# Per-engine orders from a list scheduler, separate buffers for the ternary layer, copies on ScalarE and causal masks off TensorE, in a fused attention and ternary feed-forward kernel

## Chip, cores and metric

One core of a Trainium2 chip. The metric is the device time of one execution in microseconds.

## The reference

x is 2048 rows of 256 numbers. With xn the row-normalised x, the result is x + attention(xn) + ffn(xn).

```
q, k, v   = xn @ Wq (8 heads of 32), xn @ Wk, xn @ Wv (2 key/value heads of 32); rope on q and k
out_1     = softmax(causal(q k^T / sqrt(32))) @ v
qp, kp    = q[..., :3] . dirs[h],  k[..., :3] . dirs[h]        (one number per row and head)
out_2     = softmax(causal(qp kp^T)) @ v
attention = (out_1 + head_scale[h] * (out_2 - out_1)) @ Wo

z      = xn @ ternary(W_syn)^T + b_syn          (1024 columns)
hidden = relu(z) where z >= the 102nd largest z of its row, else 0
ffn    = layernorm(xn + hidden @ ternary(W_out)^T + b_out) * gamma + beta
ternary(W) = clip(round(W / mean|W|), -1, 1) * mean|W|
```

## The kernel before

The 2048 rows are 16 tiles of 128 rows, and 4 chunks of 4 tiles. Per chunk c there is a preparation, a search for the row maxima of the scores, and the attention.

Preparation. VectorE's `row_stats` takes mean and variance of four tiles, GpSimd raises to the power -0.5 (L478), VectorE normalises (L651). Per tile TensorE transposes xn (L897), projects to q, k, v (L904), VectorE applies rope from PSUM (L679 to L688), splits q and k into a rounded and a rest part so that fast single-pass matmuls keep the precision (L693 to L706), TensorE transposes them (L909 to L915), ScalarE copies q (L567) and VectorE k (L713, L715) into the stacks. `geo` (from L720) computes running maxima for the second softmax and SP's queue spreads its rows by 16 small DMAs (L409, L412).

Maxima. The softmax needs the row maximum before the exponential. For tile t, head h, piece p a unit S computes scores of 128 rows against up to 512 keys into PSUM (L925); the last piece, which holds the diagonal, gets a further matmul that adds a mask of -1e30 (L928); VectorE reduces the unit (L745). There are 320 units, c+1 pieces for each of 8 heads and 4 tiles of chunk c. The maxima are transposed (L933) and go by DMA into a row of the q stack, so that the scores' matmul subtracts them itself.

Attention. A slot is (chunk, key/value head g, kind, key tile j): kind 0 is the first softmax, kind 1 the geometric one. Per slot TensorE computes the transposed scores of 4 heads, two pairs of PSUM banks (kind 0 at L1006, kind 1 at L1009); in a diagonal slot a mask matmul follows per head (L1013); ScalarE takes the exponential of a pair (L552) into one of two buffers `probs`; TensorE multiplies by v and by ones (L1027) into `acc`. After the last j of a kind an epilogue follows: ScalarE copies the sums (L559), VectorE the values (L770), takes a reciprocal (L772), GpSimd mixes (L503 to L510). The output projection is L984, added at L778.

Ternary layer. W_syn, later W_out, come into `z_work`, which rope's intermediates, z of tile 0 and the work space share; L785 sums |W|, L794 and L795 cut to -1, 0, 1, and the result is transposed and copied (L952, L806). Per tile t: transpose and split of xn (L956, L817, L818), z in two halves (L962 to L964), ScalarE copies with relu and sum (L582), three rounds of Sign with sum search a threshold that leaves the 102nd value within 16 ranks (L597 to L612), VectorE finds it (`select`, L825 to L834), a branch on the count of rows found (a slow path if any row missed, L857), masks (L860), transposes (L970), split (ScalarE L588, VectorE L868), down matmuls (L976, L977), layer norm on VectorE and GpSimd (L875 to L879, L523 to L529).

All units but scores and acc go through the two PSUM banks of `side`, strictly in turn: unit n uses bank n mod 2 and waits until unit n-2 has been read. `build_plan` writes one list, which every engine walks for its share in the same order. It simulates three clocks with durations written in it. `side` is a fixed list (all chunks' preparation and maxima, then weights, then the ternary layer), `slots` the attention. A side unit is placed when its bank is free on TensorE's clock plus `EARLY`, otherwise the next attention step. `blocked` holds chunk c's statistics back until chunk c-2 has been attended.

## Time and profile before

| what | us |
|---|---|
| median of 3 runs | 963.46 |
| the runs | 953.23, 963.80, 963.46 |
| profiled execution, device time | 967.53 |
| its span, first to last instruction | 965.7 |
| TensorE matmul busy | 810.1 (84%), mean granted clock 0.853 |
| TensorE weight loads | 417.4 (43%) |
| VectorE busy | 578.8 (60%) |
| ScalarE busy | 417.8 (43%) |
| GpSimd busy | 152.6 (16%) |

Busy times are sums over instructions; overlapped ones count once. Matmuls are pipelined and their ends are modelled, so the distance between two starts says more than a duration. A granted clock of 1.0 is 2.4 GHz, 0.5 is 1.2 GHz.

### The profile page before, as it was taken

Reading aid. Unit: us, or ns where it says so; the run is one execution under the profiler, and the core shown is the slowest. Engines: PE = TensorE matmul, PEld = TensorE weight load, DVE = VectorE, ACT = ScalarE, POOL = GpSimd, SP = SyncE. Lnnn points to the kernel's source line nnn. Section 1 sums busy time; section 2 is a strip of 40 time slices with the busy share of each in tenths; the row PEclk is TensorE's granted clock in tenths of the full one; section 3 lists DMA queues with packets and bytes.
Section 4 is the critical chain, followed back from the end, with each engine's and each line's share of the span. In section 5 each row is a group of like instructions: output and inputs, shape, how many; then the busy total and the mean of one; then the engine's idle time right before and its main releaser. Section 6 shows DMA issues by size and latency. Waiting matters only on the chain.

```text
span 965.7 us, 12678 instructions
## 1 busy us (share of the span) xinstructions
PE 810.1 (84%) x4916; PEld 417.4 (43%) x4916; DVE 578.8 (60%) x1139; ACT 417.8 (43%) x657; POOL 152.6 (16%) x162
## 2 busy tenths in 40 slices
PE   1677995779999997999999976889899999899643
PEld 0364554534444442543444423345445445344333
DVE  5467376675567776456587844536656654655652
ACT  0102440004543424462143352378787678676430
POOL 4000022000002002000020000200232423222443
PEclk9756797557999897998699897899899899799965
DMA  5000000000000000000000002000000000000000
GB/s 153 0 1 6 2 1 1 0 1 6 1 1 1 1 1 8 1 1 1 1 1 1 1 8 75 14 1 1 7 12 7 6 7 12 6 6 6 6 7 17
DMA packets 12436, 9.40 MB, mean 10 GB/s; under 512 B 5778, under 2 KB 11794, under 8 KB 12371
## 3 DMA queue, kind: packets, MB, share of 16 engines
q1 hardware_dynamic: 12242, 8.49, 3.0%
q8 instruction: 39, 0.64, 0.3%
q14 instruction: 27, 0.21, 0.1%
q0 software_dynamic: 128, 0.07, 0.1%
HBM read 5.80 MB, written 2.10 MB: 8 GB/s over the span
## 4 chain that ended last, share of the span: by engine, by line
PE 55%; DVE 13%; ACT 9%; issue 5%; DMA 1%; SPq 1%; POOL 0%; DVEq 0%; POOLq 0%; ACTq 0%
PE acc L1027 20%; PE side L925 10%; ACT probs L552 5%; PE scores L1006 5%; DVE piece_max L745 4%; PE scores L1009 3%; PE scores L1013 2%; PE side L984 2%; PE side L962 2%; PE side L976 2%; PE side L977 1%; PE side L963 1%; PE side L904 1%; DVE h_split L868 1%; PE side L909 1%
## 5 line engine op out<-in xcount | busy, mean ns | idle before, releaser
L552 ACT ACTIVATE probs<-scores 128x1024 f32<-128x1024 f32 (+3 forms) x320 | 275.9, 897 | 403.9 <-PE scores L1013 205.5
L745 DVE TENSOR_REDUCE piece_max<-side 128x1 f32<-128x512 f32 (+3 forms) x320 | 184.4, 607 | 79.5 <-PE side L925 47.4
L1027 PE MATMUL acc<-probs,v_nat 128*32 128x512 f32 (+3 forms) x1280 | 163.7, 585 | 12.0 <-DVE o_raw L770 8.0
L925 PE MATMUL side<-k_stack,q_stack 96*128 96x512 f32 (+3 forms) x320 | 148.0, 513 | 18.6 <-DVE piece_max L745 13.4
L1027 PE MATMUL acc<-probs,ones 128*32 128x512 f32 (+3 forms) x1280 | 159.6, 572 | 0.0
L1006 PE MATMUL scores<-q_stack,k_stack 98*128 98x512 f32 (+3 forms) x320 | 103.3, 423 | 17.3 <-DMA q_stack<-maxima 13.9
L925 PEld LDWEIGHTS side<-k_stack,q_stack 96*128 96x128 f32 x320 | 69.3, 226 | 104.9 <-DVE piece_max L745 77.4
L1006 PEld LDWEIGHTS scores<-q_stack,k_stack 98*128 98x128 f32 x320 | 56.8, 205 | 62.9 <-issue 30.8
L1009 PE MATMUL scores<-q_geo,k_geo 5*128 5x512 f32 (+3 forms) x320 | 66.1, 493 | 7.5 <-ACT probs L552 5.2
L1027 PEld LDWEIGHTS acc<-probs,ones 128*32 128x32 f32 x1280 | 36.6, 115 | 65.8 <-issue 63.4
L868 DVE TENSOR_TENSOR h_split<-side,h_split 128x512 fp32r<-128x512 f32 x32 | 20.9, 687 | 62.2 <-ACT h_split L588 61.8
L772 DVE RECIPROCAL d_raw<-d_raw 128x512 f32<-128x512 f32 x16 | 53.6, 3353 | 7.3 <-ACT d_raw L559 6.9
L1009 PEld LDWEIGHTS scores<-q_geo,k_geo 5*128 5x128 f32 x320 | 27.2, 193 | 65.7 <-issue 37.2
L1013 PE MATMUL scores<-mask_r,ident_r 128*128 128x128 f32 x256 | 53.7, 293 | 0.0
L1013 PEld LDWEIGHTS scores<-mask_r,ident_r 128*128 128x128 f32 x256 | 43.9, 203 | 13.4 <-issue 8.5
L1027 PEld LDWEIGHTS acc<-probs,v_nat 128*32 128x32 f32 x1280 | 26.4, 111 | 51.5 <-issue 38.2
L523 POOL TENSOR_TENSOR y_rstd<-y_mv,minus_half 128x1 f32<-128x1 f32 x16 | 9.0, 563 | 222.6 <-DVE y_mv L879 222.6
L567 ACT CAST q_stack<-side 96x512 fp32r<-96x512 f32 x32 | 17.6, 583 | 59.6 <-PE side L909 59.6
L507 POOL TENSOR_TENSOR o_raw<-o_raw,d_raw 128x512 f32<-128x512 f32 x8 | 10.1, 1268 | 201.9 <-DVE d_raw L772 201.9
L970 PE MATMUL side<-ident,z_work 128*128 128x128 f32 x128 | 20.6, 313 | 23.2 <-DVE z_work L860 23.2
L909 PE MATMUL side<-ident,q_nat 128*96 128x128 f32 x128 | 21.4, 321 | 22.0 <-DVE geo_nat L706 21.8
L503 POOL TENSOR_TENSOR mixed<-o_raw,d_raw 128x512 f32<-128x512 f32 x8 | 10.2, 1269 | 172.8 <-DVE d_raw L772 172.7
(166 smaller groups left out, 1068.3 us busy)
## 6 DMA issues: line engine op xcount, KB each, us to landing
res<-in_L_attn_x_dram SPq DMA_DIRECT2D x4, 512.0 KB, 7.0
out_dram<-res SPq DMA_DIRECT2D x16, 128.0 KB, 1.7
z_work<-in_L_ffn_W_syn_dram SPq DMA_DIRECT2D x1, 1024.0 KB, 5.2
z_work<-in_L_ffn_W_out_dram SPq DMA_DIRECT2D x1, 1024.0 KB, 4.8
k_geo<-geo_split SPq DMA_DIRECT2D x24, 8.0 KB
q_geo<-geo_split SPq DMA_DIRECT2D x24, 8.0 KB
w_qkv<-in_L_attn_Wq_dram SPq DMA_DIRECT2D x1, 256.0 KB, 4.4
tables<-in_cos_table_dram SPq DMA_DIRECT2D x1, 256.0 KB, 4.6
```

The lines of the kernel that those rows point to most:

```text
L552: nc.scalar.activation(probs[:, slot % 2, pair, :, off:], scores[:, pair, :, off:], ACT.Exp, scale=ATT_SCALE if kind == 0 else 1.0).then_i ...
L745: free(nc.vector.tensor_reduce(piece_max[:, h, p:p + 1], pt[:, 0:ncol], AX.X, ALU.max), a)
L772: nc.vector.reciprocal(d_raw[:], d_raw[:]).then_inc(recip_ready, 1)
L868: free(nc.vector.tensor_tensor(h_lo[:, s_], pt, h_hi[:, s_].bitcast(F32), ALU.subtract), a)
L909: last = nc.tensor.transpose(pt[0:STK, P * i:P * i + P], q_nat[:, 4 * half + i].bitcast(F32), ident[:])
L925: last = nc.tensor.matmul(pt[:, 0:ncol], q_stack[0:STK, b, h, col:col + P], k_stack[0:STK, h // HG, CHUNK * p:CHUNK * p + ncol], start=Tru ...
L962: nc.tensor.matmul(pt, xs_hi[:, i], up_T[:, i, cols], start=(i == 0), stop=False)
L970: last = nc.tensor.transpose(pt[:, P * i:P * i + P], work[:, at:at + P], ident[:])
L1006: last = nc.tensor.matmul(dst[:, off:], k_stack[:, g, P * j:P * j + P], q_stack[:, b, HG * g + h, off:], start=True, stop=not diagonal)
L1009: last = nc.tensor.matmul(dst[:, off:], k_geo[32 * h:32 * h + GROWS, g, P * j:P * j + P], q_geo[32 * h:32 * h + GROWS, b, g, off:], start= ...
L1013: last = nc.tensor.matmul(scores[:, pair, i, off:off + P], ident_r[:], mask_r[:, 0], start=False, stop=True)
L1027: last = nc.tensor.matmul(acc[D * h:D * h + D, 0 if k == "values" else 1, off:], lhs, probs[:, slot % 2, h // 2, h % 2, off:], start=first ...
```

## The change

The plan becomes one order per engine (`plan["pe"]`, `"dve"`, `"act"`, `"pool"`, `"sp"`). Work is cut into items; `add(flow, engine, rank, key, ns, after)` gives each a duration and what it needs. Items of one flow and engine keep their order, flows are free against each other. At each step the item that can start first is placed; among those of the same engine within `SLACK` ns the lowest rank wins. Attention has the lowest priority on TensorE (12, 13), picks on VectorE (4, 5); exp, cut and epilogue copies the highest on their engines. Side units take whichever bank is free first, no longer in turn, and a bank is counted with its own semaphore.

- The ternary layer gets own buffers (`z_buf` of three, `work`, `junk`), rope gets `rot` and `xnT`. W_syn is fetched right after the attention weights, ahead of the later x chunks; the layer may begin when its weights are cut.
- ScalarE takes over: the normalisation (`xn`, as scale and shift), the copies of xnT, of q's twin, of k and the geometric rows, `geo_hi`, sum of |W| (Abs with sum, in two halves), the cut weights after their transposition, `xs_hi`.
- GpSimd takes over the geometric dot products (`geo_dots`), the products of `geo_max`, and the causal cut.
- Both mask matmuls go. The scores of a diagonal slot stay unmasked and GpSimd zeroes the exponentials above the diagonal (`cut`, affine_select on 128x256, per pair); the values wait for it. The diagonal S piece is reduced by a tensor_tensor_reduce that adds `tail_mask` from SBUF.
- Values and sums are one item. Both key/value heads' geometric rows lie in one k_geo of 10 rows per head. TensorE waits for all 8 constants at the start.

```diff
-EARLY = 260
+HAND = 160
+TURN = 110
+SLACK = 120
...
+        for t in tiles:
+            old = [("unit", "qT", t - 1, 1), ("unit", "kT", t - 1)] if t else []
+            unit("qkv", 2 * c, ("xT", t), 220, [("xn", t)])
+            add("xnT", "act", 1, ("xnT", t), 400, [("unit", "xT", t)] + [("unit", "qkv", t - 1)] * (t > 0), empties=("xT", t))
+            unit("qkv", 2 * c, ("qkv", t), 1300, [("xnT", t)] + [("w",)] * (t == 0))
+            add("rope", "dve", 0, ("rope", t), 1930, [("unit", "qkv", t)] + [("q_twin", t - 1), ("geo_dots", t - 1)] * (t > 0),
+                empties=("qkv", t))
+            add("rope", "dve", 0, ("split", t), 1350, [("rope", t)] + old)
...
+                    unit("S", 2 * c + 1, ("S", t, h, p), 25 + 0.41 * cols, [("q_in", t, h // HG), ("k_in", t)])
+                    add("S", "dve", 1, ("red", t, h, p), 152 + 1.045 * cols + (20 if p == c else 0), [("unit", "S", t, h, p)],
+                        empties=("S", t, h, p))
...
+        add("pick", "dve", 5, ("pick", t, 0), 1750, [("sign", t, 2)] + [("unit", "hT", t - 1, 1)] * (t > 0))
+        add("pick", "dve", 4, ("hide", t), 2750, [("unit", "found", t)], empties=("found", t))
+        unit("h", 10, ("fo", t), 1900, [("h_lo", t, 0), ("h_lo", t, 1)] + [("w_put", 1, 3)] * (t == 0))
...
+            add("exp", "act", 0, ("exp", c, g, kind, j, pair), 170 + 855 * share, [("score", c, g, kind, j, pair)]
+                + ([("vs",) + slots[n - 2]] if n >= 2 else []))
+            if j >= TPC * c:
+                add("cut", "pool", 0, ("cut", c, g, kind, j, pair), 440, [("exp", c, g, kind, j, pair)])
...
+        add("vs", "pe", 13, ("vs", c, g, kind, j), 60 + 1700 * share,
+            [("cut" if j >= TPC * c else "exp", c, g, kind, j, PAIRS - 1)]
...
+        first = min(b[0] for b in best)
+        close = [b for b in best if b[0] <= first + SLACK and b[3] == min(best)[3]]
+        start, rank, key, eng, flow, ns, m = min(close, key=lambda b: (b[1], b[0]))
...
-                        if not full:
-                            last = nc.tensor.matmul(pt[:, col:col + P], ident_r[:], mask_r[:, 1], start=False, stop=True)
...
+                        free(nc.vector.tensor_tensor_reduce(pt[:, 0:ncol], pt[:, 0:ncol], tail_mask[:, CHUNK - ncol:], 1.0, -3.0e38,
+                                                            ALU.add, ALU.max, piece_max[:, h, p:p + 1]), ("S",) + a)
...
-                    if diagonal:
-                        for i in range(2):
-                            last = nc.tensor.matmul(scores[:, pair, i, off:off + P], ident_r[:], mask_r[:, 0], start=False, stop=True)
...
+                if k == "cut":
+                    c, g, kind, j, pair = a
+                    at = (j - TPC * c) * P
+                    tri = probs[:, slot_no[(c, g, kind, j)] % 2, pair, :, at:at + P]
+                    pool.wait_ge(probs_ready, score_no[a] + 1)
+                    nc.gpsimd.affine_select(out=tri, in_=tri, compare_op=ALU.is_ge, fill=0.0, base=0,
+                                            pattern=[[0, 2], [1, P]], channel_multiplier=-1).then_inc(cut_ready, 1)
...
+                    if j >= TPC * c:
+                        pe.wait_ge(cut_ready, cut_no[a + (PAIRS - 1,)] + 1)
+                    else:
+                        pe.wait_ge(probs_ready, score_no[a + (PAIRS - 1,)] + 1)
...
+                if k == "xn":
+                    t = a[0]
+                    act.wait_ge(shift_ready, t // TPC + 1)
+                    nc.scalar.activation(xn[:, t], res[:, t], ACT.Identity, bias=shift[:, t:t + 1],
+                                         scale=rstd[:, t:t + 1]).then_inc(xn_ready, 1)
```

## Rows read from the trace of the kernel before

**Rows 1.** Busy time by stretch; columns: stretch, length, busy by engine, granted clock, DMA.
```profile
0.00:84.00 84.00, 42.95 (x141) 29.40 (x141) 49.73 (x132) 5.93 (x9) 11.72 (x16) 0.72 0.17 45
84.00:144.00 60.00, 57.43 (x432) 32.15 (x432) 34.26 (x81) 26.08 (x41) 9.80 (x11) 0.86 0.01 3
144.00:218.00 74.00, 49.18 (x140) 32.56 (x140) 52.29 (x99) 2.29 (x4) 6.12 (x5) 0.58 0.00 1
218.00:363.00 145.00, 141.01 (x908) 65.85 (x908) 95.82 (x201) 59.72 (x76) 8.97 (x7) 0.94 0.01 2
363.00:562.00 199.00, 190.26 (x1092) 84.22 (x1096) 126.81 (x245) 77.54 (x92) 15.04 (x12) 0.88 0.01 2
562.00:608.00 46.00, 29.31 (x215) 12.41 (x208) 21.49 (x26) 17.40 (x21) 0.63 (x1) 0.83 0.16 50
608.00:910.00 302.00, 278.86 (x1902) 142.58 (x1902) 171.58 (x311) 220.20 (x398) 75.16 (x84) 0.94 0.02 6
910.00:965.70 55.70, 21.15 (x92) 18.25 (x92) 26.87 (x52) 8.63 (x18) 25.18 (x27) 0.62 0.03 10
```
**Rows 2.** The same for the tile piece_max (maxima), then probs (exponentials), then line L977.
```profile
218.00:363.00 145.00, 56.98 (x100) 0.94 0.01 2
363.00:562.00 199.00, 78.39 (x132) 0.88 0.01 2
...
608.00:910.00 302.00, 125.28 (x1024) 25.47 (x1024) 110.91 (x124) 0.94 0.02 6
...
608.00:910.00 302.00, 25.16 (x104) 19.61 (x104) 0.94 0.02 6
```
**Rows 3.** Timeline of TensorE in the attention of chunk 2: start, duration.
```profile
385.67 1.20 PE L1006 MATMUL scores<-q_stack,k_stack 98*128 98x512 f32 x4
...
388.65 1.20 PE L1006 MATMUL scores<-q_stack,k_stack 98*128 98x512 f32 x4
```
**Rows 4.** Timeline of TensorE around masks and S units in chunk 1.
```profile
341.10 0.44 PE L1013 MATMUL scores<-mask_r,ident_r 128*128 128x128 f32 x2
...
341.37 0.44 PE L925 MATMUL side<-k_stack,q_stack 96*128 96x512 f32 x1
...
344.17 0.73 PE L925 MATMUL side<-k_stack,q_stack 96*128 96x512 f32 x2
...
344.89 1.06 PE L1027 MATMUL acc<-probs,ones 128*32 128x512 f32 x8
```
**Rows 5.** Timeline of the ternary layer beside the attention of chunk 3.
```profile
650.60 0.40 PE L963 MATMUL side<-up_T,xs_lo 128*128 128x512 f32 x1
...
650.84 0.40 PE L964 MATMUL side<-b_up_r,ones_r 65*128 65x512 f32 x1
...
660.73 1.28 DVE L860 SCALAR_TENSOR_TENSOR z_work<-z_work,thresh 128x1024 f32<-128x1024 f32 x1 [1.28 <-DVEq L857]
...
663.44 1.09 PE L970 MATMUL side<-ident,z_work 128*128 128x128 f32 x8
```
**Rows 6.** Timeline of the start on VectorE, and one projection on TensorE.
```profile
9.00 8.63 DVE L651 TENSOR_SCALAR xn<-res,mean_var,rstd 128x256 f32<-128x256 f32 x4 [1.24 <-POOL rstd L478]
...
22.65 0.49 DVE L679 TENSOR_TENSOR z_work<-side,tables 128x320 f32<-128x320 f32 x1 [3.09 <-PE side L904]
...
26.04 0.42 DVE L670 COPY z_work<-side 128x256 f32<-128x256 f32 x1
```
```profile
236.75 1.56 PE L904 MATMUL side<-w_qkv,z_work 128*128 128x384 f32 x4
```
**Rows 7.** Groups of instructions by form: count, busy us, mean ns, idle before.
```profile
L772 DVE RECIPROCAL d_raw<-d_raw 128x512 f32<-128x512 f32 x16 | 53.6, 3353 | 7.3 <-ACT d_raw L559 6.9
...
L466 POOL TENSOR_SCALAR_AFFINE_SELECT xb<-xb 128x128 f32<-128x128 f32 x1 | 0.3, 292 | 0.1
```
**Rows 8.** Timeline at 910 us: VectorE and GpSimd side by side.
```profile
909.79 2.31 DVE L827 SCALAR_TENSOR_TENSOR z_work<-head_rows,search 128x1024 f32<-128x1024 f32 x1
911.10 2.13 POOL L508 TENSOR_TENSOR o_raw<-o_raw,mixed 128x512 f32<-128x512 f32 x1
```

More of the change, by code:

```diff
@@ L88, in build_plan, with add, unit @@
-    alone = {"stats": 3500, "geo": 8500, "mx": 200, "weigh": 4600, "select": 7200}
-    def up(t):
-        return [("up_xs", t), ("up_z", t)]
-    side = []
+    op, queue, ranks = {}, {}, {}
+    def add(flow, eng, rank, key, ns, after=(), mode=None, empties=None):
+        op[key] = (eng, ns, tuple(after), mode, empties)
+        ranks[key] = rank
+        queue.setdefault((eng, flow), []).append(key)
+    def unit(flow, rank, name, ns, after=()):
+        add(flow, "pe", rank, ("unit",) + name, ns, after, "full")
@@ new lines, in build_plan @@
+    for t in range(NT):
+        unit("o", 0, ("o", t), 860, [("mix", t // TPC, G - 1, 1)])
+        add("o", "dve", 0, ("o_add", t), 430, [("unit", "o", t)], empties=("o", t))
+        add("dma", "sp", 0, ("store", t), 500, [("o_add", t), ("y_out", t)])
+    done = {("x", c): 6000 + 1500 * c for c in range(NCH)}
+    done.update({("w",): 9000, ("late",): 14000, ("w_in", 0): 12000, ("w_in", 1): 13000})
+    emptied_by = {}
+    for key, o in op.items():
+        if o[4]:
+            emptied_by.setdefault(o[4], []).append(key)
@@ new lines, in build_plan @@
+    gates = {}
+    for name, keys in emptied_by.items():
+        own, seen = ("unit",) + name, list(keys)
+        for r in seen:
+            seen += [d for d in op[r][2] if d in op and own in op[d][2] and d not in seen]
+        gates[own] = tuple(d for r in seen for d in op[r][2] if d != own and d not in seen)
+    bank = {}
+    holds = [None] * BANKS
+    clock = {e: 0.0 for e in ("pe", "dve", "act", "pool", "sp")}
+    mode = "full"
+    heads = {q: 0 for q in queue}
+    plan = {e: [] for e in clock}
@@ L469, in late_constants @@
[L469 to L490 removed]
+            constant(nc.gpsimd.memset(ones, 1.0))
@@ L1025, in _ @@
-                    for h in range(HG):
-                        lhs = v_nat[:, j, g] if k == "values" else ones[:, 0:D]
-                        last = nc.tensor.matmul(acc[D * h:D * h + D, 0 if k == "values" else 1, off:], lhs,
-                                                probs[:, slot % 2, h // 2, h % 2, off:], start=first, stop=end)
-                    if k == "sums":
-                        last.then_inc(probs_used, 1)
+                    if j >= TPC * c:
+                        pe.wait_ge(cut_ready, cut_no[a + (PAIRS - 1,)] + 1)
+                    else:
+                        pe.wait_ge(probs_ready, score_no[a + (PAIRS - 1,)] + 1)
@@ L1034 @@
+                    if first and e >= 1:
+                        pe.wait_ge(raw_ready, 2 * e)
+                    for part, lhs in enumerate((v_nat[:, j, g], ones[:, 0:D])):
+                        for h in range(HG):
+                            last = nc.tensor.matmul(acc[D * h:D * h + D, part, off:], lhs,
+                                                    probs[:, slot % 2, h // 2, h % 2, off:], start=first, stop=end)
+                    last.then_inc(probs_used, 1)
 _INS = ["L0_attn_x", "L0_attn_Wq", "L0_attn_Wk", "L0_attn_Wv", "L0_attn_Wo", "L0_attn_head_scales", "L0_ffn_W_syn",
```

1078 lines of the change are left out of this document (586 added, 492 removed).

## The prediction

> **What bounds the kernel now.** I read the stretches first. The cuts are mine: 84 us is where the first attention score starts, 144, 363 and 608 lie where the attention of chunk 0, 1 and 2 ends or the next can begin, 910 is the last reciprocal. TensorE shows as busy 810 of 965.7 us, but its instructions are long for two reasons: where the granted clock is low (0.58 to 0.72 of a stretch, a mean of its levels of 1.2 and 2.4 GHz) many take twice as long, and beside other work a matmul's latency is counted as busy. Three things stand out [rows 1].
>
> First, attention is absent for long. It starts at 84 us; from 144 to 218 us ScalarE works for 2.3 us, since the attention of chunk 1 waits for its row maxima and TensorE (clock 0.58) only feeds the reductions; from 562 to 608 us the weights of the ternary layer are fetched and cut; from 910 to 966 us three tiles of the ternary layer go through one after the other, TensorE busy 21 us, clock 0.62. Second, the ternary layer starts only at 608 us: 104 of the 128 down matmuls of one line, 13 of the 16 tiles, lie between 608 and 910, on top of the longest attention [rows 2]. Third, VectorE is busy 579 us, spread at 60% over all of it: the maxima alone are 57 and 78 us in 218-363 and 363-562, 21.4 more for each chunk of 32 more pieces of 512 columns, so 36 in the stretch before and 0.67 us a piece [rows 2]. No engine is full; the order of the work is what costs time. So I price what each stretch needs on each engine, and ask what the new order lets lie side by side.
>
> **Unit prices at full clock.** A full attention slot of kind 0 (scores, values, sums) repeats after 388.65 - 385.67 = 2.98 us; kind 1 has cheaper scores, I take 2.6, so 2.8 on average [rows 3]. Diagonal slots counted by columns, chunk c has 4(4c+2.5) full slots: 10, 26, 42, 58, or 28, 73, 118 and 162 us. Two S units and a mask take 344.89 - 344.17 = 0.72 us with both changes of shape, so 0.3 us a unit without mask [rows 4]; 32, 64, 96, 128 units are 10, 19, 29, 38 us. A projection is 1.56 us, and with its ten transposes (eight take 1.1 us) a tile's preparation is 2.9, a chunk 11.5 us [rows 5, 6]. A ternary tile: ten 512-column matmuls each 0.24 us after the last, eight transposes, and 16 down matmuls of half the columns at 0.12, with xsT 5.7 us [rows 5]. Output projection about 3.5 us a chunk (16 matmuls of 256 columns and 4 passes each).
> VectorE: preparation of a tile 26.04 - 22.65 = 3.4 us, chunk 13 [rows 6]; maxima 15, 36, 57, 78 us; each epilogue 3.35 for the reciprocal and 0.7 for the copy, 16 us a chunk [rows 7]; a ternary tile (171.6 - 16)/13 = 12 us in 608-910 plus 1.3 us standing at the branch [rows 1, 5], so 13.3.
>
> **The edits.** *Masks off TensorE.* Two diagonal masks cost 341.37 - 341.10 = 0.27 us [rows 4], so the 256 are 35 us at full clock; with the 128 S masks about 45. Below: nothing, where VectorE is late; above: twice that at half clock, 90. I take them out by using prices without masks (8 to 10 us a chunk). In return VectorE adds a mask inside the diagonal reduction. The trace has no such instruction; nearest is a reduction of the same PSUM tile, so plus nothing; far bounds are a gain of nothing and the reciprocal's 3353/512 = 6.5 ns a column [rows 7]: 40,960 columns by 5.2 ns more than a piece's 1.3 are 215 us. I take nothing, since two-operand PSUM instructions run like one-operand ones (0.49 us for 320 columns) [rows 6].
> *Cut on GpSimd.* 128 selections of 128x256 on the exponentials. The mask builder takes 0.29 for 128x128 [rows 7]; so 0.3 to 0.6 each, I take 0.45 and 58 us in all. It lies between exp and values in 64 diagonal slots. With two probs buffers the other slot covers it if GpSimd is free; uncovered it is 64 x 0.6 = 38 us. In front of it on GpSimd may stand a mix of four operations (5.7 us) or y_out (4.5); this I keep as a rival.
> *Copies to ScalarE.* Some six 128x256 copies a tile at 0.42 [rows 6] are 40 us, and weights, geometry and small products 30 more: VectorE falls from 579 to about 510, ScalarE rises from 418 to some 470, GpSimd from 153 to about 245. ScalarE has the room: in 608-910 it needs 110.9 for exp and (220.2 - 110.9)/13 = 8.4 a tile [rows 1, 2], so 196 of 245 us after the change. SP's queue gains W_syn ahead of the later x chunks: 5 us, hidden, as these chunks are wanted after 60 us. Values and sums in one item: two changes of shape fewer per slot (up to 160 x 0.2 = 32 us), but VectorE may stand 0.5 us more behind each; I take zero.
>
> **Sum by stretch.**
> Start to first score, 84: the first transpose waits until about 18, because the four normalisations took 8.63 us, where four instructions of the size of L670's 0.42 are 1.7, while GpSimd filled memory [rows 6]; these go to ScalarE and the big fill is late, so first matmul near 11. Tiles overlap (own buffers), 6 us instead of 8 a tile, and the maxima of tile 0 start before tile 3 is ready. 84 - 7 - 8 - 11 = 58.
> 84-218, 134 us: VectorE needs 13 + 36 + 16 + 8 (geometry, statistics) = 73, TensorE 28 + 19 + 11.5 = 59. VectorE bound: 78.
> 218-363, 145 us: TensorE 73 + 29 + 11.5 + 3.5 = 117, VectorE 57 + 13 + 16 + 8 = 94. Two ternary tiles fit: TensorE 128, VectorE 121: 130.
> 363-608, 245 us: TensorE 118 + 38 + 11.5 + 3.5 = 171, VectorE 115, room for four tiles: 194, at clock 0.95: 204.
> 608-910, 302 us: 162 + 3.5 + ten tiles 57 = 223, at 0.95 and 4% of waits: 245.
> Tail, 56 us: reciprocal 3.4, mix 5.7, four projections 3.5, add, store and what the last tile lags: 22.
> 58 + 78 + 130 + 204 + 245 + 22 = 737 us of span. The orders are fixed per engine by a plan at full clock with a hand-over of 160 ns, and the chip's clock will differ; a queue that waits in order loses some of it: 11 us. With 2 us around the span that is **750 us**. The profiled execution took 967.5 (span 965.7), the runs shown have a median of 963.5, 0.4% less; I let that stand inside the range.
>
> **A rule that speaks against the change.** At 909.79 VectorE's L827 with two SBUF inputs took 2.31 us beside GpSimd's L508 with 2.13 [rows 8], against 1.28 of VectorE's L860 of the same form [rows 5]: about 1 us lost per collision. This kernel puts 92 us more on GpSimd. The Trainium skill (SBUF — State Buffer, "Who interferes with whom") says a VectorE instruction with two SBUF inputs and a GpSimd instruction that reads SBUF exclude one another for the whole instruction; by that rule the trace agrees, and nearly every cut that meets a pick waits for it.
>
> **Rivals.**
> *Gaps close, stretches don't shrink* (25%). For: in 218-562 TensorE already shows 331 of 344 us busy, and each S unit between attention matmuls costs two changes of shape; static orders drift. Against: VectorE is busy there only 65%, and there are masks to save. 60 + 90 + 145 + 215 + 290 + 22 = 822 us.
> *TensorE truly full* (11%). 381 + 96 + 46 + 91 + 14 + 6 = 634 us at full clock, 21 of it in the first 58: 58 + 613 + 22 = 693 us. Against: a clock of 0.94 even in the fullest stretches.
> *GpSimd collides* (6%), the mechanism of rows 8: 128 cuts by 1 us, half of it uncovered, 64 us: 814 us, from one collision in two cuts on.
> *GpSimd sets the end* (3%), slower. Every diagonal slot's values stand on TensorE's queue behind a cut that stands behind mix, y_out or the fill; TensorE's queue goes in order, so scores, S units and the ternary layer wait too. It passes 985 us from (985 - 750)/64 = 3.7 us a slot on; with a mix ahead of each (5.7) it is 750 + 64 x 5.7 = 1115. Against: the longest queue item must precede nearly every cut, and the plan counts GpSimd.
> *The masked reduction is slow* (3%): at the far bound 215 us more on VectorE, a quarter in each chunk; half of it hidden: 860 us. The change would then not relieve the path where it says so.
>
> **How the numbers follow.** Forecast 52%, own range 705 to 795. The rest as above. Two in ten are left out below 685 and above 835, so the range is 685 to 835. A measurement tells about 2% from no change. Faster by over 2% (below 944) 94%, within 2% 3%, slower 3%.
>
> **What would show it.** Right: the first score near 58 us; no stretch of tens of us without exp before the tail; ternary tiles finished before the attention of chunk 3; granted clock above 0.9 from 60 us on; VectorE near 510 us, busy about 70%; no mask matmuls; tail near 20 us. The masked reduction of 512 columns near 0.69 us and cuts near 0.45 on GpSimd. Wrong: long waits of the values matmuls for the cuts, more ternary tiles behind the end of attention, exp waiting in order behind sign or copies, or TensorE standing behind the two shared PSUM banks.

## The result: faster by 9.5%, under half of the forecast gain

The changed kernel takes 869.57 us (median of four runs, 867.40 to 876.45), beside 963.63 us for the kernel before (median of four, 953.23 to 966.24): a ratio of 0.905, interval 0.898 to 0.912. The forecast was 750 us, 685 to 835. The direction was right, the size was not. The profiled execution took 870.59 us (span 868.7). The ratios of the experiments below go by fast runs alone: beside experiments 1, 3, 5 and 6 two of the seven runs of the kernel before counted as slow, and these four comparisons are on record as unclear at 2%.

The stretches of the kernel after, with the columns of [rows 1]. The cuts lie at the first score (100), and where exp is absent for long: 154 to 208, 314 to 361, 531 to 572, and from 816 on.

```profile
0.00:100.00 100.00, 58.19 (x178) 33.85 (x179) 60.02 (x177) 28.03 (x59) 22.26 (x44) 0.78 0.21 60
100.00:154.00 54.00, 47.96 (x355) 23.07 (x354) 35.12 (x71) 36.30 (x72) 29.28 (x58) 0.84 0.00 1
154.00:208.00 54.00, 39.53 (x112) 19.44 (x109) 43.15 (x100) 3.46 (x9) 8.62 (x12) 0.59 0.01 4
208.00:314.00 106.00, 103.42 (x742) 45.80 (x740) 60.10 (x129) 63.44 (x91) 28.66 (x56) 0.97 0.01 2
314.00:361.00 47.00, 39.01 (x104) 18.14 (x105) 38.47 (x76) 4.06 (x10) 7.35 (x11) 0.56 0.01 1
361.00:531.00 170.00, 166.33 (x1123) 70.69 (x1121) 97.33 (x193) 97.40 (x133) 32.37 (x59) 0.96 0.01 2
531.00:572.00 41.00, 30.83 (x123) 17.80 (x122) 29.21 (x51) 3.96 (x9) 7.01 (x7) 0.67 0.02 5
572.00:816.00 244.00, 235.15 (x1703) 114.49 (x1705) 130.38 (x240) 207.25 (x372) 86.82 (x108) 0.97 0.02 7
816.00:868.70 52.70, 23.01 (x120) 18.90 (x109) 28.70 (x51) 10.79 (x25) 21.37 (x23) 0.62 0.03 11
```

Read it in pairs. Wherever attention runs from 208 us on, TensorE is busy 96% or more and its clock is at 0.96 or 0.97. Between, three times, ScalarE does 3.5 to 4 us of work in 41 to 54 us and the clock is 0.56 to 0.67: 142 us in all. Before, there were two such holes, 74 and 46 us [rows 1]. The one at 144 shrank to 54; the one of the weights at 562 went; but a new one stands at 314, and one at 531 in its place. The tail is 53 us, as before.

What is in the holes? The maxima's matmuls (L1078, before L925), by the same stretches (first the kernel after from 154 on, then the kernel before from 144 on):

```profile
154.00:208.00 54.00, 30.25 (x52) 0.59 0.01 4
208.00:314.00 106.00, 19.72 (x55) 0.97 0.01 2
314.00:361.00 47.00, 27.44 (x41) 0.56 0.01 1
361.00:531.00 170.00, 40.14 (x104) 0.96 0.01 2
531.00:572.00 41.00, 14.80 (x26) 0.67 0.02 5
```
```profile
144.00:218.00 74.00, 35.06 (x64) 0.58 0.00 1
218.00:363.00 145.00, 38.41 (x96) 0.94 0.01 2
363.00:562.00 199.00, 56.28 (x128) 0.88 0.01 2
```

Before, all 96 units of chunk 2 and all 128 of chunk 3 lay beside the attention of the chunk ahead of it. In the changed order the attention runs out first: 55 units of chunk 2 lie beside it and 41 behind it, alone, at 0.67 us each (27.44/41) instead of 0.36 (19.72/55). Where the ternary layer went is seen by its down matmuls, 16 a tile (the windows of the tile down_T):

```profile
361.00:531.00 170.00, 2.14 (x16) 1.96 (x16) 0.00 (x0) 0.96 0.01 2
...
572.00:816.00 244.00, 23.42 (x176) 21.76 (x176) 0.00 (x0) 0.97 0.02 7
816.00:868.70 52.70, 11.26 (x48) 10.46 (x48) 0.00 (x0) 0.62 0.03 11
```

One tile by 531 and one more by 572, eleven in 244 us, three in the tail. The forecast had six before chunk 3.

Groups of the page after: busy us, mean ns, then the idle time before them and what ended it.

```profile
PE 743.4 (86%) x4536; PEld 362.2 (42%) x4536; DVE 522.5 (60%) x1086; ACT 454.7 (52%) x773; POOL 243.7 (28%) x374
...
L894 DVE TENSOR_REDUCE piece_max<-side 128x1 f32<-128x512 f32 x192 | 128.7, 687 | 61.3 <-PE side L1078 60.0
L1176 PE MATMUL acc<-probs,v_nat 128*32 128x512 f32 (+3 forms) x1280 | 159.0, 570 | 3.2 <-POOL probs L575 3.0
...
L575 POOL TENSOR_SCALAR_AFFINE_SELECT probs<-probs 128x256 f32<-128x256 f32 x128 | 55.6, 448 | 166.9 <-ACT probs L696 165.7
...
L897 DVE CUSTOM_DVE_ANT_0 side<-side,tail_mask 128x128 f32<-128x128 f32 (+3 forms) x128 | 62.7, 496 | 34.9 <-PE side L1078 34.4
```

The loads came out as priced: VectorE 522 us (510 forecast), ScalarE 455 (470), GpSimd 244 (245). The values waited 3.0 us in all for cuts. The loads of these three engines were not what went wrong.

### The profile page after: what moved, and what is told of

Read it like the earlier page. It is cut to its first block, busy times and chain, and to the rows that moved or that the text cites. A ratio compares the mean times of both kernels' runs of the same rounds, so it can differ in the third digit from the quotient of the medians.

```text
span 868.7 us, 12439 instructions
## 1 busy us (share of the span) xinstructions
PE 743.4 (86%) x4536; PEld 362.2 (42%) x4536; DVE 522.5 (60%) x1086; ACT 454.7 (52%) x773; POOL 243.7 (28%) x374
## 4 chain that ended last, share of the span: by engine, by line
PE 60%; DVE 10%; issue 4%; ACT 4%; POOL 3%; DVEq 0%; POOLq 0%; ACTq 0%
PE acc L1176 26%; PE side L1078 10%; PE scores L1156 6%; DVE piece_max L894 4%; PE scores L1160 4%; ACT probs L696 2%; PE side L1122 2%; PE side L1131 2%; PE side L1114 2%; PE side L1132 2%; PE side L1055 1%; PE side L1115 1%; DVE side L897 1%; PE side L1139 1%; PE side L1061 1%
## 5 line engine op out<-in xcount | busy, mean ns | idle before, releaser
L1078 PE MATMUL side<-k_stack,q_stack 96*128 96x512 f32 (+3 forms) x320 | 154.6, 548 | 24.0 <-DVE piece_max L894 14.6
L894 DVE TENSOR_REDUCE piece_max<-side 128x1 f32<-128x512 f32 x192 | 128.7, 687 | 61.3 <-PE side L1078 60.0
L1176 PE MATMUL acc<-probs,ones_all 128*32 128x512 f32 (+3 forms) x1280 | 152.8, 550 | 0.0
L1078 PEld LDWEIGHTS side<-k_stack,q_stack 96*128 96x128 f32 x320 | 69.4, 232 | 123.3 <-DVE piece_max L894 46.2
L575 POOL TENSOR_SCALAR_AFFINE_SELECT probs<-probs 128x256 f32<-128x256 f32 x128 | 55.6, 448 | 166.9 <-ACT probs L696 165.7
L897 DVE CUSTOM_DVE_ANT_0 side<-side,tail_mask 128x128 f32<-128x128 f32 (+3 forms) x128 | 62.7, 496 | 34.9 <-PE side L1078 34.4
L1176 PEld LDWEIGHTS acc<-probs,ones_all 128*32 128x32 f32 x1280 | 43.0, 115 | 82.8 <-issue 80.0
L1160 PE MATMUL scores<-q_geo,k_geo 10*128 10x512 f32 (+3 forms) x320 | 54.3, 473 | 10.0 <-ACT probs L696 10.0
L1131 PE MATMUL side<-down_T,h_split 128*128 128x256 f32 x128 | 36.7, 318 | 8.5 <-DVE h_split L1022 8.5
L1160 PEld LDWEIGHTS scores<-q_geo,k_geo 10*128 10x128 f32 x320 | 21.8, 186 | 48.5 <-ACT probs L696 30.6
L1055 PE MATMUL side<-w_qkv,xnT 128*128 128x384 f32 x64 | 33.9, 666 | 6.3 <-DVE xs_lo L959 3.5
L782 ACT CAST h_split<-side 128x512 fp32r<-128x512 f32 x32 | 18.2, 591 | 38.7 <-PE side L1122 38.5
```

What stands on the lines that cost most here:

```text
L575: nc.gpsimd.affine_select(out=tri, in_=tri, compare_op=ALU.is_ge, fill=0.0, base=0, pattern=[[0, 2], [1, P]], channel_multiplier=-1).then_ ...
L894: free(nc.vector.tensor_reduce(piece_max[:, h, p:p + 1], pt, AX.X, ALU.max), ("S",) + a)
L897: free(nc.vector.tensor_tensor_reduce(pt[:, 0:ncol], pt[:, 0:ncol], tail_mask[:, CHUNK - ncol:], 1.0, -3.0e38, ALU.add, ALU.max, piece_max ...
L1055: last = nc.tensor.matmul(pt[:, 0:QKV], xnT[:, i], w_qkv[:, i], start=(i == 0), stop=(i == KC - 1))
L1078: last = nc.tensor.matmul(pt[:, 0:ncol], q_stack[0:STK, b, h, col:col + P], k_stack[0:STK, h // HG, CHUNK * p:CHUNK * p + ncol], start=Tru ...
L1131: nc.tensor.matmul(pt[:, 0:C], h_hi[:, i], down_T[:, i], start=(i == 0), stop=False)
```

## The experiments

Fourteen kernels ran, each beside the kernel before on its chip. Ratios are against that one. Where an edit adds or drops lines, the line numbers of its profile are off by one or two. The edits are shown in part; "..." marks what is left out.

**1. Values and sums as two items again.** An edit of the change that its forecast had at zero.

```diff
-        add("vs", "pe", 13, ("vs", c, g, kind, j), 60 + 1700 * share,
+        add("vs", "pe", 13, ("va", c, g, kind, j), 30 + 850 * share,
...
+        add("vs", "pe", 13, ("vs", c, g, kind, j), 30 + 850 * share, [("va", c, g, kind, j)], "columns")
...
```

> Values and sums become two items again, so that S units can be put between them; everything else as in the changed kernel. Theory A (two side banks hold 1.4 us of reductions, the merged item of values and sums keeps TensorE for 1.9 us, so VectorE stands still behind each of them and the maxima of the next chunk are not ready when the attention ends): VectorE's share in the stretches 208-319 and 361-534 rises above 70%, the three stretches without exponentials (154-208, 319-361, 534-572) shrink by 10 to 20 us each, total 825 to 845 us. Theory B (the loss is elsewhere, and more changes of shape on TensorE only cost): each slot pays about 0.2 us more, 160 slots, total 880 to 905 us.

828.52 us, ratio 0.859 (0.848 to 0.870): 41 us less than the changed kernel. The stretches, same columns (the last one is the attention of chunk 2); then its maxima's matmuls alone:

```profile
157.00:201.00 44.00, 33.26 (x92) 14.99 (x92) 36.21 (x82) 2.77 (x7) 7.12 (x7) 0.57 0.01 1
201.00:321.00 120.00, 118.72 (x767) 50.43 (x766) 75.13 (x161) 63.72 (x92) 29.43 (x59) 0.95 0.01 2
321.00:352.00 31.00, 25.32 (x94) 13.20 (x91) 24.68 (x46) 2.88 (x7) 7.35 (x11) 0.61 0.01 2
352.00:537.00 185.00, 184.04 (x1197) 76.75 (x1196) 115.92 (x233) 106.96 (x159) 34.74 (x61) 0.99 0.01 3
```
```profile
201.00:321.00 120.00, 28.91 (x76) 0.95 0.01 2
321.00:352.00 31.00, 13.12 (x20) 0.61 0.01 2
```

Beside the attention of chunk 1 now lie 76 units instead of 55, 20 are left over, the third hole is gone, and the tail (804 to 825 us) is 21 us, because the ternary layer is done with the attention. The hole at 321 shrank by 16 us, but the attention ahead of it grew by 14 (120 us against 106), so there almost nothing is won. The gain, 44 us between the profiled spans, lies elsewhere: 7 us up to the attention of chunk 1, 26 from the start of chunk 2's attention to that of chunk 3 (185 us against 211), and 9 in chunk 3's attention and tail together (288 against 297).

**2. Two items in the plan, but issued as one.** Experiment 1's order, with the sums moved right behind their values on TensorE.

```diff
+    for key in plan["pe"]:
+        if key[0] != "vs":
+            order.append(key)
+        if key[0] == "va":
+            order.append(("vs",) + key[1:])
```

> The order is planned as in the version with values and sums as two items (828.5 us), but on TensorE the sums then always follow right behind their values, eight matmuls in a row. Theory G (the grain on the chip counts: eight matmuls in a row make every side unit that waits behind them up to 0.8 us later, hence VectorE too): the gain of the split is lost, 860 us or more. Theory O (the gain came from the order that the plan finds when it counts two short items: the preparation and the maxima of the next chunk are placed earlier among the slots): the gain stays, 825 to 840 us, with the gaps of exp near 157-201 and 321-352 us as in that version.

843.20 us, ratio 0.880 (0.872 to 0.889), between the two theories: of the 41 us some 26 come from the order that the planner finds with short items, 15 from the shorter grain on the chip. Both are differences of medians; by the ratios they are 24 and 20, so each is known to some 5 us.

**3. The weights of the ternary layer late.** Rank 9 instead of 0, so they no longer go ahead of chunk 0's preparation.

```diff
-        unit("w", 0, ("wsum", m), 60, [("w_abs", m)])
+        unit("w", 9, ("wsum", m), 60, [("w_abs", m)])
...
-            unit("w", 0, ("wT", m, i), 440, [("w_cut", m)])
+            unit("w", 9, ("wT", m, i), 440, [("w_cut", m)])
```

> Rank of the sums and transpositions of the ternary weights on TensorE from 0 to 9, behind preparation and maxima. Theory W (the first score comes at 99.7 us because the weights' cuts, transpositions and copies stand between the tiles of chunk 0): first score 10 to 18 us earlier, and the whole kernel 5 to 15 us shorter, 855 to 865 us, since VectorE has the same work to do later. Theory C (the start is bound by the chain of preparation at the low clock): first score moves by less than 5 us and the time stays within 3 us of 870.

865.39 us, ratio 0.898 (0.888 to 0.908): the first exp comes at 88.4 instead of 100.7 us, but only 4 us of this, no more than the intervals leave open, reach the end. The last exp comes at 791 instead of 816, and the tail grows to 72 us at a clock of 0.66, four tiles in it.

**4. Both of 1 and 3.**

> Values and sums as two items and the weights' rank 9, both edits of the first two experiments. If the two gains are independent (theory A and W each remove their own idle time): about 828 - 4 to 828 - 12, 815 to 825 us, first score near 88 us and a tail below 30 us. If the late weights only move the ternary layer to the end (the tail of 73 us that they left alone): 828 us or more.

819.76 us, ratio 0.851 (0.846 to 0.856). The best version of the study; it beats both kernels. The first score comes at 85.9 us. The stretches of its first hole and of the attention of chunks 2 and 3, same columns:

```profile
142.00:200.00 58.00, 46.32 (x144) 24.22 (x136) 40.08 (x94) 7.24 (x16) 9.10 (x14) 0.59 0.01 1
...
336.00:530.00 194.00, 190.78 (x1213) 80.44 (x1212) 114.16 (x232) 105.94 (x156) 31.25 (x61) 0.97 0.01 2
530.00:800.00 270.00, 261.83 (x1842) 127.63 (x1845) 174.36 (x321) 223.72 (x408) 111.80 (x132) 0.97 0.02 7
```

Two more numbers of the planner turned on top (`SLACK` 160, the reciprocals' rank 3.5) changed nothing:

> As before with SLACK 160 for 120 and the reciprocal's rank 3.5 for 2, behind the maxima. If the reciprocals of 3.35 us in front of reductions hold the banks: 5 to 10 us below the run with both edits, 808 to 820 us. If not: the same within 4 us.

820.43 us, ratio 0.856 (0.849 to 0.862).

**5. The ternary layer first**: ahead of the maxima of chunks 2 and 3, a rough way to get the tiles that the forecast wanted early. Its other units on TensorE change rank in the same way.

```diff
-            unit("z", 11, ("z", t, half), 1180, [("xs_lo", t)] + ([("w_put", 0, 3), ("b_split",)] if t == 0 else []))
+            unit("z", 4.5, ("z", t, half), 1180, [("xs_lo", t)] + ([("w_put", 0, 3), ("b_split",)] if t == 0 else []))
...
-        unit("h", 10, ("fo", t), 1900, [("h_lo", t, 0), ("h_lo", t, 1)] + [("w_put", 1, 3)] * (t == 0))
+        unit("h", 4.4, ("fo", t), 1900, [("h_lo", t, 0), ("h_lo", t, 1)] + [("w_put", 1, 3)] * (t == 0))
```

> Ranks of the ternary layer's two flows on TensorE from 11 and 10 to 4.5 and 4.4, ahead of preparation and maxima of chunks 3 and of S in chunk 2. Theory F (my forecast: VectorE has room for six ternary tiles before the attention of chunk 3, only the ranks keep them out): many tiles done by 500 us, the attention of chunk 3 about as early, total 800 to 840 us. Theory S (side banks and VectorE's time are what the maxima need; each ternary tile put ahead costs its whole 13 us there): the attention of chunk 3 starts 100 us later or more, total above 940 us.

1018.62 us, ratio 1.057 (1.047 to 1.068): slower than before. Its last stretches:

```profile
594.00:829.00 235.00, 159.40 (x419) 89.22 (x416) 147.55 (x303) 45.33 (x107) 35.95 (x52) 0.54 0.01 3
829.00:1020.00 191.00, 173.22 (x1295) 62.18 (x1293) 17.88 (x12) 115.43 (x132) 26.17 (x42) 0.94 0.03 9
```

Nine tiles are masked by 528 us, but chunk 3's maxima are late for it: 235 us without attention at a clock of 0.54, and then 171 us of attention (the last exp ends at 1000 us) and the tail with nothing beside them, VectorE busy 18 us.

**6. Is it the cut?** Cuts left out, so the exponentials above the diagonal stay in the sums.

```diff
-                    nc.gpsimd.affine_select(out=tri, in_=tri, compare_op=ALU.is_ge, fill=0.0, base=0,
-                                            pattern=[[0, 2], [1, P]], channel_multiplier=-1).then_inc(cut_ready, 1)
+                    pool.nop().then_inc(cut_ready, 1)
```

> GpSimd's 128 causal cuts become empty instructions with the same waits and signals, so the diagonal blocks are not masked: this part of the computation is left out. Theory G (the cuts, or GpSimd behind them, hold the values on the path): 25 us or more less, below 845 us. Theory H (the second probs buffer hides them): 3 to 12 us less, 858 to 867 us.

870.06 us, ratio 0.905 (0.896 to 0.914): 55 us of GpSimd's work less (188.3 of the page against 243.7) and no difference. VectorE is as busy as with the cuts, 522.4 us against 522.5.

**7. Is it the masked reduction?** Here the diagonal pieces are reduced plainly; the mask of the maxima is left out.

```diff
-                        free(nc.vector.tensor_tensor_reduce(pt[:, 0:ncol], pt[:, 0:ncol], tail_mask[:, CHUNK - ncol:], 1.0, -3.0e38,
-                                                            ALU.add, ALU.max, piece_max[:, h, p:p + 1]), ("S",) + a)
+                        free(nc.vector.tensor_reduce(piece_max[:, h, p:p + 1], pt[:, 0:ncol], AX.X, ALU.max), ("S",) + a)
```

> The reduction of the diagonal S pieces takes no mask any more (plain tensor_reduce over the same columns), the order unchanged; the causal mask of the maxima is left out, so a row's maximum may come from a key it does not see. VectorE loses the accumulator reads (128 x 0.14 = 18 us) and nothing else. Theory V (VectorE's time sets the stretches without exponentials): 8 to 18 us less than the changed kernel, 853 to 862 us. Theory P (TensorE's or the bank's hand-over sets them): under 5 us less, above 865 us.

873.48 us, ratio 0.907 (0.902 to 0.913): no difference. But it took less from VectorE than expected: its busy time fell by 5 us (517.8 against 522.5) and not by 18, since most of a separate read lies over the end of its reduction. So this run says little about VectorE, and the next one tests it.

**8. Is it VectorE at all?** Every reduction reads the first half of its columns and adds no mask; the other half of the maxima is left out.

```diff
-                        free(nc.vector.tensor_reduce(piece_max[:, h, p:p + 1], pt, AX.X, ALU.max), ("S",) + a)
+                        free(nc.vector.tensor_reduce(piece_max[:, h, p:p + 1], pt[:, 0:CHUNK // 2], AX.X, ALU.max), ("S",) + a)
```

> The changed kernel with every reduction of the maxima reading only the first half of its columns and adding no mask: half of the maximum is left out, some 111 us of VectorE's work go (70 thousand columns of 1.3 ns, 90 us, and the 18 us of separate reads with the mask). Theory V (the stretches without exp wait for VectorE's reductions): the three stretches without exp, 142 us together, shrink by a third or more and the time is under 830 us. Theory R (a unit's round trip through its bank sets the pace there, matmul at the low clock, hand-over, reduction, hand-over, two banks): they shrink by under a fifth, 845 to 865 us. Theory P (the order alone counts, the engines have room): within 1% of 869.6 us.

839.46 us, ratio 0.881 (0.873 to 0.890). VectorE's busy time fell by 74 us (448.6 of the page against 522.5), less than the 111 expected, since a reduction of half the columns takes 0.42 us and not half of 0.69. The time fell by 30 us (by the ratios 23), and the three holes from 142 to 125 us: under a fifth, as Theory R has it, though the whole time fell more than it said. Why a hole hardly shrinks is seen in the timeline. First the changed kernel, then this one, both where units run alone:

```profile
170.51 1.11 PE L1078 MATMUL side<-k_stack,q_stack 96*128 96x512 f32 x2 [0.57 <-DVE piece_max L894]
...
171.41 0.69 DVE L894 TENSOR_REDUCE piece_max<-side 128x1 f32<-128x512 f32 x1 [0.28 <-PE side L1078]
172.01 0.56 DVE L897 CUSTOM_DVE_ANT_0 side<-side,tail_mask 128x384 f32<-128x384 f32 x1
172.15 1.22 PE L1078 MATMUL side<-k_stack,q_stack 96*128 96x512 f32 x2 [0.53 <-DVE piece_max L894]
```
```profile
162.19 1.12 PE L1077 MATMUL side<-k_stack,q_stack 96*128 96x512 f32 x2 [0.27 <-DVE piece_max L894]
163.02 0.42 DVE L894 TENSOR_REDUCE piece_max<-side 128x1 f32<-128x256 f32 x1 [0.62 <-PE side L1077]
163.36 0.35 DVE L897 TENSOR_REDUCE piece_max<-side 128x1 f32<-128x192 f32 x1
...
163.50 1.12 PE L1077 MATMUL side<-k_stack,q_stack 96*128 96x512 f32 x2 [0.20 <-DVE piece_max L894]
```

A pair of units goes through the two banks every 1.64 us (172.15 - 170.51). With 0.5 us less of reductions it is 1.31 us (163.50 - 162.19), and what is left is the pair's matmuls, 1.12 us at a granted clock of 0.50, and a hand-over. At 0.3 us a unit, the price in the forecast, it would be 0.6.

**9. The units preferred more**, values and sums still one item. In a hole the attention has run out; so the planner's preference is raised for TensorE alone.

```diff
-        close = [b for b in best if b[0] <= first + SLACK and b[3] == min(best)[3]]
+        close = [b for b in best if b[0] <= first + (400 if min(best)[3] == "pe" else SLACK) and b[3] == min(best)[3]]
```

> The changed kernel with one number of the planner raised for TensorE alone: a unit of a lower rank is preferred when it can start within 400 ns of the first item (120 before). Values and sums stay one item. In TensorE's order of the changed kernel 50, 39 and 22 of the maxima's units of chunks 1, 2 and 3 stand behind the last slot of the chunk before; here 42, 2 and 0, near the split version's 40, 16 and 0. Theory O (what costs is that units are left over when the attention runs out, and the merged item costs by that): the stretch without exp near 314 us shrinks from 47 to under 15 us, that near 531 goes, and the time is 810 to 835 us. Theory M (the merged item costs on the chip by its length, whatever the order): those stretches shrink, but the attention is stretched by as much, 850 us or more.

852.63 us, ratio 0.882 (0.878 to 0.885), 17 us less. The hole at 314 fell from 47 to 24 us and the one at 531 is gone, but the attention of chunk 1, 208.7 to 337.3 us, takes 129 us instead of 106 with nearly the same number of matmuls (747 against 742), as Theory M had it. The tail is 19 us, although values and sums are still one item.

So holes went by 62 us (142 to 80) and the time by 17: a hole is half a symptom. It costs only as far as what lies in it would otherwise run beside something else without making that longer.

**10. The same on the best version**, at 600 and then at 300 ns.

> The best version so far (values and sums two items, the ternary weights' flow late, 819.8 us) with the same number at 600 ns: no unit of the maxima is left behind the attention of the chunk before (42, 4 and 0 there). Theory O: the stretch without exp near 142-200 us goes too, and the time falls by 10 to 40 us, to 780-810 us. Theory F (that stretch is filled only by holding the little attention of chunk 0 back, since VectorE needs 64 reductions, four tiles of rope and two reciprocals there in any order): exp becomes sparse before instead, and the time is the same within 10 us.

963.81 us, ratio 1.000 (0.997 to 1.004). Neither theory: all that the change had brought is lost. The units come early and the ternary layer too (last mask at 750 us), but the attention is held back for them. There are three stretches without exp again, from 146, 252 and 473 us on, 176 us in all at a clock of 0.53 to 0.55, and at the end the attention is what is left over:

```profile
252.00:313.00 61.00, 55.00 (x114) 23.82 (x110) 48.85 (x109) 3.12 (x5) 0.64 (x3) 0.55 0.00 1
...
473.00:555.00 82.00, 69.75 (x144) 31.22 (x144) 64.97 (x130) 3.22 (x4) 0.00 (x0) 0.54 0.00 0
...
755.00:942.00 187.00, 169.81 (x1184) 52.25 (x1182) 13.38 (x10) 104.29 (x120) 24.36 (x43) 0.97 0.00 1
```

In the 187 us a slot of kind 0 repeats every 3.84 us, not 2.98 [rows 3]:

```profile
879.82 0.73 PE L1157 MATMUL scores<-q_stack,k_stack 98*128 98x512 f32 x2 [0.18 <-ACT probs L697]
...
881.67 1.94 ACT L697 ACTIVATE probs<-scores 128x1024 f32<-128x1024 f32 x2 [1.91 <-PE acc L1178]
...
883.66 0.73 PE L1157 MATMUL scores<-q_stack,k_stack 98*128 98x512 f32 x2 [0.18 <-ACT probs L697]
```

That nothing lies beside it is not the reason. The slot of [rows 3] stands alone too, and so does the attention that experiment 5 left over, where the same matmuls repeat every 2.98 us (850.58 - 847.60):

```profile
847.60 1.19 PE L1156 MATMUL scores<-q_stack,k_stack 98*128 98x512 f32 x4
...
850.58 1.20 PE L1156 MATMUL scores<-q_stack,k_stack 98*128 98x512 f32 x4
```

The orders differ. In experiment 5 TensorE's list has the scores of a slot, then values and sums of the slot before it. At 600 ns it has the scores of a slot, then the sums of the slot before the last one, then the values of the last one. The exp writes the `probs` buffer that those late sums still read, so it waits for them (1.91 us a slot), and the next scores wait for the exp. The clock is full and TensorE reads as busy 91%, and still part of this is waiting. But the loss is not there: against experiment 4 the attention of chunk 3 takes 49 us less (722 to 942 us, against 532 to 800), and what lies between the first exp of chunk 1 and the first of chunk 3 takes 200 us more (190 to 722 us, against 200 to 532).

> The best version (819.8 us) with the preference for units at 300 ns instead of 120, between that version and the one with 600 ns (963.8 us). In TensorE's order 34, 0 and 0 of the maxima's units stand behind the attention of the chunk before, against 42, 4 and 0. Theory O (fewer units left over is better as long as the attention is not starved): 800 to 820 us. Theory G (every unit preferred delays the attention, which then lacks company at its end): 825 us or more, with slots that repeat every 3.8 us and nothing beside them at the end.

830.94 us, ratio 0.861 (0.853 to 0.869). Of the holes only the first, 145 to 196 us, remains, and the time is 11 us more than with the hole at 320. Theory G has the size; but its slots of 3.8 us didn't come: at the end, where kind 1 runs alone, a slot repeats every 2.9 us, as kind 1 does at 600 ns; in experiment 5, with values and sums as one item, it is 2.3.

**11. The transfers of the maxima first.** SP issues 16 small transfers of chunk 0's geometric rows from 87.95 us on and the maxima behind them, though these are done at 89.86 us:

```profile
96.75 1.36 SPq L474 DMA_DIRECT2D q_stack<-maxima  x2
```

```diff
+    plan["sp"].remove(("m_dma", 0))
+    plan["sp"].insert(plan["sp"].index(("geo_dma", 0)), ("m_dma", 0))
```

> The changed kernel with two entries of SP's list swapped: the maxima of chunk 0 go out before the 16 small transfers of the geometric rows. In the changed kernel VectorE has finished the maxima at 89.86 us, SP issues geometric rows from 87.95 to 96.7 and the maxima's two transfers at 96.75, the first score starts at 99.72. Theory Q (the queue's order holds the first score back): the first score starts near 93 us, and the time falls by 4 to 8 us. Theory N (something else is needed at that place anyway, or the gain is lost later): the first score moves, the time is the same within 3 us.

876.65 us, ratio 0.909 (0.901 to 0.917), no gain. The transfers are issued at 86.16, but the first score moves only from 99.72 to 97.04, and nothing is waited for just ahead of it. Even these 2.7 us are not the edit's: in this profiled execution TensorE was 3.7 us earlier already at the last unit of chunk 0 (79.79 against 83.53), which lies ahead of the edit.

```profile
97.04 0.71 PE L1158 MATMUL scores<-q_stack,k_stack 98*128 98x512 f32 x2
```

In TensorE's list the score stands behind part of the preparation of chunk 1 and z of tile 0, which were put there while the plan thought it late. The 12 us by which the late weights moved the first exp are therefore, for the most part, not SP's order.

**12. What the masks on TensorE had cost.** The kernel before without its 384 mask matmuls; the causal masking is left out.

```diff
-                    if diagonal:
-                        for i in range(2):
-                            last = nc.tensor.matmul(scores[:, pair, i, off:off + P], ident_r[:], mask_r[:, 0], start=False, stop=True)
...
```

> The kernel before without its 384 mask matmuls, order unchanged: causal masking is left out. Theory M (they cost what their spacing shows, 0.27 us for two): 25 to 50 us less, 915 to 940 us. Theory N (they hide in waits for exponentials and reductions): under 15 us less, above 950 us. My forecast of the change counted 45 us at full clock for them.

948.68 us, ratio 0.989 (0.981 to 0.997): some 11 us, where 45 had been counted. TensorE's busy time did fall by 43 us (767.1 of the page against 810.1). The hole ahead of chunk 1's attention kept its length, 76.9 us without exp against 77.6, and its clock, 0.60 against 0.58: what its units no longer spend on masks is waited.

## Why the forecast was wrong, by its own steps

| stretch of the forecast | forecast | changed kernel | experiment 4 |
|---|---|---|---|
| start to first score | 58 | 100 | 86 |
| to the attention of chunk 1 | 78 | 108 | 114 |
| to that of chunk 2 | 130 | 153 | 136 |
| to that of chunk 3 | 204 | 211 | 194 |
| that of chunk 3 | 245 | 244 | 270 |
| tail | 22 | 53 | 21 |
| drift | 11 | in the rows | in the rows |
| span | 748 | 869 | 821 |

**"Values and sums in one item ... I take zero"** was the costliest step that an experiment priced: 41 us (experiments 1 and 2). The forecast looked at two changes of shape and at VectorE standing 0.5 us, so at what the item itself takes. What counts is that a list of big items gives the small ones between them fewer turns. In the kernel after, a pair of units at 268.88 is followed by the next at 272.19, behind a slot's scores, values and sums. VectorE comes to the first pair late, after a reciprocal, but is done with both at 271.5 and stands for 1.19 us:

```profile
268.88 0.61 PE L1078 MATMUL side<-k_stack,q_stack 96*128 96x128 f32 x2
...
270.34 1.07 PE L1176 MATMUL acc<-probs,v_nat 128*32 128x512 f32 x8
...
271.22 1.04 PE L1176 MATMUL acc<-probs,ones_all 128*32 128x512 f32 x8
...
272.19 0.57 PE L1078 MATMUL side<-k_stack,q_stack 96*128 96x512 f32 x2
...
272.73 0.69 DVE L894 TENSOR_REDUCE piece_max<-side 128x1 f32<-128x512 f32 x1 [1.19 <-PE side L1078]
```

The attention of the chunk is then over with 41 units undone. The tail goes by the order too: with two items it is 21 us, as forecast, and 19 with one item and the units preferred (experiment 9).

**The unit of 0.3 us** was the step under it. The prices of TensorE hold where work is mixed: in 208-314 lie the attention of chunk 1 (73 us by the forecast), 55 units (16.5), three projections with their transposes (8.7) and thirteen matmuls of the output projection (2.9), 101 of 106 us. They don't hold where units are alone: then two banks, the low clock and the hand-overs make it 0.8 us a unit (1.64 / 2). The sum by stretch took the larger of each engine's load and so let every unit lie beside something.

**"VectorE bound: 78"** for 84-218 fell for that reason. VectorE's load was nearly right, 73 us in its sum: 35 + 43 = 78 us in 100-208 after. But it took 108, in experiment 4 it is 77 in 114. VectorE's load doesn't set it: with a part of it gone (experiment 8) the hole went from 54 to 49.5 us. There is too little attention in chunk 0 (28 us) to lie beside chunk 1's preparation and 64 units.

**"84 - 7 - 8 - 11 = 58"** is off by 42. The first matmul came at 13.2 instead of 11. Tiles didn't follow every 6 us: rope starts at 19.1, 26.4, 36.5 and 45.7. The split of a tile stands until the last transposes of the tile ahead have read the one buffer:

```profile
42.19 0.29 DVE L854 CAST q_nat<-rot 128x256 fp32r<-128x256 f32 x1 [4.06 <-PE side L1069]
```

and a projection (L1055) takes TensorE 2.9 us, four times, instead of 1.56 [rows 6]. The granted clock is 0.50 at the fourth, at 42.77. For the three ahead of it, at 14.31, 21.68 and 33.55, the trace has no record of the clock (its first is at 36.8 us), so that it was low there too is argued from the same duration and not shown. The kernel before has such a projection as well, 2.93 us at 19.61. Then the weights, 12 us of it by experiment 3; and the 32 units of chunk 0, which the forecast let start beside the preparation: all but one run alone from 63.0 to 85.2 us. Fourteen us more pass until the first score (experiment 11).

**"Two ternary tiles fit ... room for four tiles".** No: one tile by 531. TensorE is busy 103 of 106 and 166 of 170 us there with only this one. The room that the forecast saw was TensorE's time at the price of 0.3 for every unit. Putting the layer ahead of the maxima (experiment 5) costs 149 us; whether a few tiles fit in a gentler order was not tried. The attention of chunk 3 itself came out as priced, though, eleven tiles instead of ten in 244 us, and fifteen in 270 in experiment 4.

**Masks, 45 us**: 11 (experiment 12). The sum was a little off, since 384 masks at half of 0.27 us are 52. But the load was not the mistake, 43 us of TensorE's busy time went. The step that failed was to take a load off TensorE as time off the kernel: the masks lay for the most part where TensorE waited anyway. The lower bound given was nearer.

**What held.** The masked reduction was priced like a plain one: 699 ns for 512 columns, of plain ones 687. Not in the forecast was a separate read of the result, 0.14 us each; most of it lies over the end of the reduction, so that mask and reads together add 5 us to VectorE's busy time, and they cost nothing (experiment 7). The cut: 448 ns forecast as 0.45, hidden (experiment 6). So neither *GpSimd collides* nor *GpSimd sets the end* nor *the masked reduction is slow* happened. Half of the cuts took 408 ns or less and the longest 1417; the difference of mean and median, 40 ns by 128, is an estimate of 5 us for all that collisions did to them. The rule weighed in the forecast, of the Trainium skill (SBUF — State Buffer, "Who interferes with whom"), that a VectorE instruction with two SBUF inputs and a GpSimd one that reads SBUF exclude one another, has little to act on here: for the cuts the trace shows no more than these 5 us, eight of 128 took over 0.5 us, and without them neither VectorE's busy time nor the kernel's time changed (experiment 6). The nearest rival was *gaps close, stretches don't shrink*, 822 us. The opposite happened: the stretches of attention did shrink, and holes opened between them.

Of the 121 us between forecast and span, the start is 42, the next two stretches 53, the tail 31, chunk 3's approach 7; the 11 of drift go off. Experiment 4 wins back 48, and of the 73 that it still lacks 64 lie ahead of 200 us; 25 more lie in the attention of chunk 3, which has fifteen tiles beside it instead of ten, and other stretches and the drift give 16 back. Not tried: more than two banks for the units, a second buffer for the split rows, and a plan whose durations know the low clock; so what these 64 us would give is open.

## What to carry to other kernels

Before summing an engine's load over a stretch, ask whether there is something to lie beside each part of it, and price what is left over by what it takes alone (here 0.8 us a unit instead of 0.3). A list scheduler is as sensitive to the grain of the items as to their order: cut the long item of the low-priority flow short, and count in each engine's finished list how many items of the next stage stand behind the last of this one. Preference helps only up to a point: 400 ns won 17 us, 600 ns on the best version lost 144, by holding the attention back. And look at the order inside a slot that the scheduler repeats: an item that frees a buffer and comes one slot late makes the slot 3.84 us instead of 2.98.

## What the runs showed of the hardware

That an engine can read as busy 91% at a full clock with waits inside: in experiment 10 the matmuls of a slot repeat every 3.84 us, in experiment 5 the same matmuls every 2.98, at a busy share of 91% and 97% over the stretch (169.81 of 187 us, 166.14 of 171).
